# Longer flights of gathers, and the wait for a row slot one gather earlier

## What is computed

```python
e = jnp.stack([tbl_0[ids[:, 0]], ..., tbl_31[ids[:, 31]]], axis=1)     # 2048 x 32 x 64
p = x[:, row_idx, :]; q = x[:, col_idx, :]                             # x = e, all i < j
kp = jnp.einsum('bpe,fpe,bpf->bp', p, kernel, q)                       # 2048 x 496
h = jnp.concatenate([z, dense_ctx], axis=1)
h = jnp.maximum(h @ W_top1 + b_top1, 0.0)
h = jnp.maximum(h @ W_top2 + b_top2, 0.0)
y = h @ W_top3
```

## Time and profile before

| what | value |
|---|---|
| time, median of 3 runs | 920.49 us (919.31 to 921.08) |
| time of the profiled execution | 920.72 us |
| its span (first to last instruction) | 918.9 us |
| PE busy | 772.1 us (84%) |
| DVE busy | 653.4 us (71%) |
| ACT busy | 644.8 us (70%) |
| POOL busy | 483.8 us (53%) |
| mean granted PE clock | 0.937 |

### The profile page before, as it was taken

The page is one execution under the profiler, slowest core; times in us unless marked ns, Lnnn a source line. Parts: engine busy times, 40 slices in busy tenths (PEclk is TensorE's granted clock), DMA queues, the critical chain, the costliest instruction groups (busy, mean ns, idle before and its releaser), DMA issues.

```text
span 918.9 us, 16548 instructions
## 1 busy us (share of the span) xinstructions
PE 772.1 (84%) x4672; PEld 314.0 (34%) x4672; DVE 653.4 (71%) x601; ACT 644.8 (70%) x5196; POOL 483.8 (53%) x518
## 2 busy tenths in 40 slices
PE   0489949788688899999647596899699999999998
PEld 0245525355333233333212132233233333333333
DVE  0478949589566777999645385779677898888960
ACT  0288949867348628799653196789757799999962
POOL 6666666666666666555555555555555555520000
PEclk9989979799889999999977798999899999999999
DMA  9511111211212121111211121111112111100100
GB/s 339 155 34 35 36 35 23 46 23 35 47 23 46 24 47 23 32 33 20 45 21 41 20 44 20 22 20 42 21 20 44 44 21 44 19 13 1 24 2 0
DMA packets 34644, 36.40 MB, mean 40 GB/s; under 512 B 18676, under 2 KB 20980, under 8 KB 34424
## 3 DMA queue, kind: packets, MB, share of 16 engines
q0 software_dynamic: 16384, 16.81, 10.2%
q1 hardware_dynamic: 18168, 18.53, 6.8%
HBM read 26.91 MB, written 0.01 MB: 29 GB/s over the span
## 4 chain that ended last, share of the span: by engine, by line
PE 51%; POOL 23%; DMA 11%; issue 10%; ACT 3%; DVE 2%; DVEq 0%; POOLq 0%
POOL rows L392 17%; PE y_ps L492 15%; PE y_ps L514 13%; PE sum_ps L528 10%; DMA rows<-tbl_dram,idx 10%; POOL kept_rows L392 6%; PE layer_ps L544 3%; ACT batch_products L654 3%; PE layer_ps L547 2%; PE y_ps L450 2%; DMA kept_rows<-tbl_dram,idx 2%; PE y_ps L507 1%; PE y_ps L561 1%; PE y_ps L495 1%; DVE products L737 1%
## 5 line engine op out<-in xcount | busy, mean ns | idle before, releaser
L654 ACT ACTIVATE batch_products<-batch_products 128x64 f32<-128x64 f32 x2576 | 615.3, 242 | 165.0 <-DVE batch_products L748 164.9
L392 POOL DMA_INDIRECT rows<-tbl_dram,idx x384 | 362.3, 943 | 248.5 <-issue 95.1
L654 ACT ACTIVATION_READ_ACCUMULATOR batch_products<-batch_products 128x1 f32 x2576 | 485.6, 189 | 0.0
L737 DVE TENSOR_TENSOR products<-y_ps,xt 128x1024 f32<-128x1024 f32 (+1 forms) x224 | 255.6, 1198 | 55.2 <-PE y_ps L493 48.3
L748 DVE TENSOR_TENSOR batch_products<-y_ps,kept_rows 128x1024 f32<-128x1024 f32 x192 | 225.7, 1218 | 31.7 <-PE y_ps L516 24.8
L514 PE MATMUL y_ps<-kernel_sb,xt 64*128 64x512 f32 x384 | 207.6, 673 | 4.4 <-DVE products L729 2.3
L492 PE MATMUL y_ps<-xt,kernel_sb 64*128 64x512 f32 (+1 forms) x448 | 208.4, 600 | 0.4 <-DVE products L737 0.3
L493 PE MATMUL y_ps<-xt,kernel_sb 64*128 64x512 f32 (+1 forms) x448 | 208.3, 600 | 0.0
L516 PE MATMUL y_ps<-kernel_sb,xt 64*128 64x512 f32 x384 | 207.6, 673 | 0.0
L528 PE MATMUL sum_ps<-products,selector 128*32 128x512 f32 (+1 forms) x1520 | 159.9, 534 | 4.3 <-ACT z_sb L624 1.7
L392 POOL DMA_INDIRECT kept_rows<-tbl_dram,idx x128 | 120.9, 944 | 80.4 <-issue 34.2
(11 more groups left out here) (54 smaller groups left out, 440.8 us busy)
## 6 DMA issues: line engine op xcount, KB each, us to landing
kernel_sb<-pair_kernel_dram SPq DMA_DIRECT2D x15, 512.0 KB, 11.2
rows<-tbl_dram,idx POOLq DMA_INDIRECT x384, 2.4
special<-xt SPq DMA_DIRECT2D x48, 128.0 KB
kept_rows<-tbl_dram,idx POOLq DMA_INDIRECT x128, 2.5
special<-xt SPq DMA_DIRECT2D x32, 64.0 KB
w_sb<-w_dram SPq DMA_DIRECT2D x1, 1024.0 KB
w_sb<-w_dram SPq DMA_DIRECT2D x1, 512.0 KB
kernel_sb<-pair_kernel_dram SPq DMA_DIRECT2D x1, 256.0 KB, 3.2
```

Source lines behind the costliest of these rows:

```text
L392: pool.indirect_dma_start(rows_of(g, q, t)[:, h, :], None, tables[j], bass.IndirectOffsetOnAxis(ap=idx[:, n, j:j + 1], axis=0)).then_inc(l ...
L654: last = nc.scalar.activation(product, product, ACT.Copy, accum_out=batch_sums(unit)[:, column:column + 1])
L737: nc.vector.tensor_tensor(into[:, :, 0:size], y[:, :, 0:size], by, ALU.mult).then_inc(unit_done, 1)
```

## The change

Flights become longer: in segments 0 and 1 a flight opens at every fourth pair (16 gathers), in chunk 1 at every second pair (16 gathers), in chunks 2 and 3 at every pair (8 gathers). The wait for the slot of a pair no longer stands at that pair's first gather but at the last gather (half 1, last tile) of the pair ahead of it. For kept rows of chunks 2 and 3 it stands once, for pair 0, instead of once for each of pairs 0 to 3.

```diff
--- before.py
+++ after.py
@@ -105,11 +105,15 @@
           + [(3, 0, kb) for kb in range(2)])
 GROUPS = 7
 FIELDS = [(g, q, h) for g in range(len(SEGMENTS)) for q in range(PAIRS) for h in range(2)]
+
+
 def opens_flight(field):
     g, q, h = field
     if half(g):
+        return h == 0 and q % 4 == 0
+    if chunk(g) == 1:
         return h == 0 and q % 2 == 0
-    return h == 0 or chunk(g) > 1
+    return h == 0
 
 
 FLIGHT = [n for n, field in enumerate(FIELDS) if opens_flight(field)]
@@ -369,19 +373,28 @@
             pool.wait_ge(identity_cleared, 1)
             nc.gpsimd.affine_select(out=identity[:], in_=identity[:], compare_op=ALU.not_equal, fill=1.0, base=0,
                                     pattern=[[-1, P]], channel_multiplier=1).then_inc(identity_made, 1)
+
+            def pair_behind(g, q):
+                return (g, q + 1) if q + 1 < PAIRS else (g + 1, 0)
+
+            def wait_for_slot(g, q):
+                if g == len(SEGMENTS):
+                    return
+                c, ahead = chunk(g), first_of(chunk(g)) - 1
+                if q == 0 and c >= 2:
+                    pool.wait_ge(unit_done, max(UNIT_OF[unit] for unit in BATCH if chunk(unit[1]) == c - 2) + 1)
+                elif q >= KEPT + ROW_RING:
+                    pool.wait_ge(unit_ready, TURN_OF[g, q - ROW_RING] + 1)
+                elif q >= KEPT and c:
+                    pool.wait_ge(unit_ready, TURN_OF[ahead, q - ROW_RING + PAIRS - KEPT] + 1)
+
             for g in range(len(SEGMENTS)):
-                c, before = chunk(g), first_of(chunk(g)) - 1
+                c = chunk(g)
                 if g == 0:
                     pool.wait_ge(ids_landed[0], 16)
                 elif g == first_of(1):
                     pool.wait_ge(ids_landed[1], 16)
                 for q in range(PAIRS):
-                    if q < KEPT and c >= 2:
-                        pool.wait_ge(unit_done, max(UNIT_OF[unit] for unit in BATCH if chunk(unit[1]) == c - 2) + 1)
-                    elif q >= KEPT + ROW_RING:
-                        pool.wait_ge(unit_ready, TURN_OF[g, q - ROW_RING] + 1)
-                    elif q >= KEPT and c:
-                        pool.wait_ge(unit_ready, TURN_OF[before, q - ROW_RING + PAIRS - KEPT] + 1)
                     for h in range(2):
                         j = 2 * q + h
                         if (g, q, h) in LANDED_FIRST:
@@ -389,6 +402,8 @@
                             pool.wait_ge(landed(*of[:2]), landed_by(*of))
                         for t in tiles(g):
                             n = c * TILES + t
+                            if h == 1 and t == tiles(g)[-1]:
+                                wait_for_slot(*pair_behind(g, q))
                             pool.indirect_dma_start(rows_of(g, q, t)[:, h, :], None, tables[j],
                                                     bass.IndirectOffsetOnAxis(ap=idx[:, n, j:j + 1], axis=0)
                                                     ).then_inc(landed(g, q), 16)
```

## The result

The changed kernel takes **840.51 us** (median of 4 runs, 839.88 to 841.0), where the kernel before takes 919.9 beside it (919.21 to 921.08). The ratio is 0.9135, with a 95% interval of 0.912 to 0.9151. The forecast was 846, in a range of 835 to 866. This holds for chips on which the kernel before takes 920 us. On the two chips of the last four experiments it takes 1008 and 1037 us; on the second the changed kernel was run again and loses time; on the first only two kernels near to it were run, and they lose time too. The last experiments are about that.

The account below looks back on a forecast made before the run. PE was taken to follow POOL's gathers up to chunk 2's last pair. Savings of 30.0 + 19.5 + 13.5 + 3 = 66 us there and 8.4 at chunk 3's pair 4 made the span 844.5, the time about 846 us; range 835 to 866.

Parts of the forecast that it names:

- Which bound: Up to chunk 2's last pair PE waits for POOL's gathers; from there PE's own dense work sets the end.
- Fewer openings: Up to chunk 2's last gather 31 of 61 openings go: 30.0 us (landing alone) and 19.5 us (with slot wait).
- the moved slot wait: 26 of the 30 openings that stay lose the slot wait, 13.5 us; at its new place it costs nothing.
- Rival B: The slot wait's half microsecond stays, at the opening or its new place: 859.8 us, 855 to 864; chance 0.18.
- The estimate from the Trainium skill: A 32 KB gather lands in 2.1 us, each opening removed saves 0.4 us less, and the end comes at 858 us.
- Long gaps: Of about 6 us in single long POOL gaps ahead of chunk 2's last gather, 3 us go (bounds 0 and 6).
- The clock: PE's granted clock: nothing counted for shorter waits; behind 531 us a microsecond or two may come back.
- Left waiting: PE's waits for DMA stay near 58 us: 31 at the start and 27 behind.
- C: Rival: PE's waits turn into waits for ACT's batch sums, half the gain is lost, 884 us; chance 0.11.
- D: Rival: the moved slot wait binds, nearest at chunk 3's end, and the kernel is slower, about 1010 us; chance 0.03.
- E: Rival: no change in time, as the landings would have to be hidden anyway; chance 0.02.

Follow-up runs that it names:

- the last four experiments: Kernel before without landing waits: 1269.44 us; changed kernel with 4-gather flights in chunk 3 from pair 5: 1169.43, again 1202.87; changed kernel unaltered: 1248.95.
- the first experiment: The changed kernel's longer flights alone, with the slot wait left at the opening as in the kernel before: 857.27 us, ratio 0.932.

## Why the prediction was right, and where it was off

*Which bound.* PE followed POOL up to chunk 2's last pair, and PE's own work was behind it. Shown by the turn and the gather that both moved by 68.3 us, and from the other side by putting openings back up to chunk 1 (all of 23.6 us come through).

*Fewer openings and the moved slot wait*, 30.0 + 19.5 + 13.5 = 63.0 us. The gaps are those assumed: 1.64 to 1.89 at 41 of 46, 0.30 at the slot wait's new place. Apart, the halves brought 53.3 (52.5 reckoned, with 3 for long gaps) and 19.8 us. Rival B, that the half microsecond stays, is what the kernel of the first experiment is: 857.27, in B's range of 855 to 864. The moved wait costs nothing, as forecast from the wait inside a flight; but the half microsecond did not come of having two waits. It came of the late one standing alone ahead of the gather, and no row that I had read showed that. The estimate from the Trainium skill, "DMA: Bandwidth & Descriptors", Anatomy of one DMA (858 for the end), would have each opening save 0.4 us less; the changed kernel came to 840.5, and the gaps of 1.75 against 0.30 bear the rows out.

*Long gaps.* The term of the sum was 3 us in bounds of 0 to 6; what is left of the 68.3 is 5.3, so nearly all of those ahead of chunk 2's last gather went (chunk 1's first opening among them, from 3.21 to 2.30). **Mis-sized by 2.3 us.**

*The clock.* "I count nothing; behind it a microsecond or two may come back" was the largest miss: **4.1 us** came behind chunk 2's last turn, 1.9 before chunk 3's pair 4 and 2.2 after it. The experiment with openings put back in chunk 3 shows the 2.2 to belong to the wait of 8 us: it comes and goes with it. The 1.9 rests on the window rows above: the kernel before works 3.4 us of that stretch at half the clock, right behind its wait of 4.55, which costs about 1.7; the changed kernel, after a wait of 0.41, has no such window. No experiment takes that wait away alone. The two make the 6.4 us between the forecast span of 844.5 and the measured 838.1; the median lies 2.4 us over that span where 1.5 were added, so 5.5 are left between 846.0 and 840.5.

*Left waiting.* 27 us behind the first 34 were forecast, 38.4 measured. PE's busy time fell from 772.1 to 753.0 us, only 3.8 of these 19.1 behind chunk 2's last turn (1.9 in either window); what PE gained ahead of it, where POOL sets the pace, turned into waiting and made the end no earlier.

*Rivals.* C: DVE waited 7.0 us for ACT's sums, against 5.7, so ACT caught up with nothing that mattered. D: no gather of the changed kernel waited for a turn for longer than its 0.30, and the last gather came at 710.06 where 712 was reckoned. With flights of two pairs the moved wait does bind, for 6.48 us and at the place that D named, the last gather of chunk 3's pair 14; the time was the expected one all the same (828.31 us for 829). E fell with the result. But a slower outcome exists that none of the rivals had: on one chip the changed kernel takes 21% more than the kernel before, and on another a version with more landing waits than it takes 16% more. I gave slower 0.03 for another reason, the slot wait; that without landing waits the other engines can come to stand stood nowhere in the trace of a chip where they don't.

## What to carry to other kernels

Where one engine feeds another, sum up its serial time only to the last place where the other still waits: an opening taken out ahead of it is worth its whole 1.45 us, and behind it PE's own work sets the end. If an instruction has two waits, let the one that ends last be the instruction's own, here by naming it first in the program; the other way round cost 0.5 us each time. And before waits that look useless are taken out of a stream of gathers, try it on several chips, on those above all where the kernel is already slow: the same edit brought 8.7% on one and cost 21% on another.

## What the runs showed of the hardware that was not expected

- The order of two waits ahead of one gather decides 0.5 us. With the late wait named second in the program it is 0.76 us from the landing to the gather, at all 52 such openings of the kernel before; with it named first 0.26, and the time falls from 920.16 to 898.64 us for that swap alone.
- With no landing waits at all 512 gathers of 32 KB, 1.25 us apart, land as fast as with them on a chip at 920: median 2.5 us, longest 5.8.
- A wait of PE of 8 us cost 2.2 us more in the work behind it, by the clock: PE worked for 4.5 us at a granted clock of 0.50.
- On two of the four chips of the experiments kernels with fewer drains are slower: 1248.95 against 1036.75 us for the kernel that takes 840.5 against 920 elsewhere, and 1269.44 against 1008.19 us with the landing waits alone taken out. In the trace of the first, increments of PE's semaphore reach DVE up to 57 us after the matmul's end, and PE and ACT get one instruction in 1.4 to 2.1 us.
